# Attention and feed-forward sandwich on one core: batch 0's key and query writes reordered, one load group put behind a small copy, projections and casts spread over the first blocks

## What is computed

```python
x = x + layernorm(attention(layernorm(x)))
x = x + layernorm(ffn(layernorm(x)))

def attention(x):            # 16 heads of 8 features
    q = x @ Wq + bq
    k = (x @ Wk + bk) @ Wl + bl
    v = (x @ Wv + bv) @ Wl + bl
    p = softmax(q @ k.T / sqrt(8))        # per head, 512 x 512
    return (p @ v) @ Wo + bo

def ffn(x):                  # x_prev: the tokens moved down by one
    xr, xk = mix(x, x_prev, mu_r), mix(x, x_prev, mu_k)
    return sigmoid(xr @ W_r) * (square(relu(xk @ W_k)) @ W_v)
```

## Time and profile before

| | us |
|---|---|
| median of 3 executions | 261.02 (260.88 to 261.04) |
| the profiled execution | 260.82 |
| its span in the trace | 259.0 |
| PE busy in the span | 243.8 (94%) |
| DVE busy | 201.7 (78%) |
| ACT busy | 176.5 (68%) |
| POOL busy | 97.2 (38%) |

### The profile page before, as it was taken

One profiled execution on the slowest core, in us unless ns is written; L12 is line 12 of the kernel. 1 busy time (PEld: TensorE's weight loads), 2 busy tenths in 40 slices (PEclk: granted clock), 3 DMA queues, 4 the chain that ended last, 5 costly groups with the idle time before them and its releaser, 6 DMA issues.

```text
span 259.0 us, 4266 instructions
## 1 busy us (share of the span) xinstructions
PE 243.8 (94%) x1359; PEld 91.7 (35%) x1359; DVE 201.7 (78%) x363; ACT 176.5 (68%) x344; POOL 97.2 (38%) x228
## 2 busy tenths in 40 slices
PE   8999979999999999999999999999999999899980
PEld 3554432223222242234322522343224323332560
DVE  3795988778888799879699899796898997721665
ACT  2565868778776866787677767866777677686122
POOL 5948772010101105641216255512153545117322
PEclk9999999999999999999999999999999999999997
DMA  5345765303030303030304130303031000000101
GB/s 162 86 141 158 210 177 168 87 9 93 2 95 2 92 9 87 4 89 4 91 4 94 42 91 4 91 2 94 4 91 42 3 2 0 7 0 0 43 0 41
DMA packets 13816, 15.68 MB, mean 61 GB/s; under 512 B 3153, under 2 KB 11346, under 8 KB 13794
## 3 DMA queue, kind: packets, MB, share of 16 engines
q1 hardware_dynamic: 13218, 15.15, 21.6%
q10 hardware_dynamic: 576, 0.26, 0.4%
HBM read 11.01 MB, written 4.19 MB: 59 GB/s over the span
## 4 chain that ended last, share of the span: by engine, by line
PE 78%; DVE 10%; issue 3%; POOL 3%; ACT 2%; DMA 1%; POOLq 0%; DVEq 0%; ACTq 0%
PE psO L1327 23%; PE psB L1315 21%; PE psA L1296 18%; DVE mx L957 6%; PE psM L1210 3%; PE psM L1216 2%; PE psM L1196 2%; DMA x_all<-in_L_attn_x_dram 1%; PE psO L1234 1%; PE psM L1243 1%; POOL mm L509 1%; PE psM L1276 1%; PE psA L1196 1%; PE psB L1505 1%; PE psM L1256 1%
## 5 line engine op out<-in xcount | busy, mean ns | idle before, releaser
L957 DVE TENSOR_REDUCE mx<-psA 128x2 f32<-128x1024 f32 x128 | 151.1, 1219 | 31.0 <-PE psA L1296 30.6
L809 ACT ACTIVATE pT<-psB 128x512 f32<-128x512 f32 x244 | 132.9, 596 | 39.9 <-PE psB L1315 39.6
L1315 PE MATMUL psB<-QS,KS 75*128 75x512 bf16 x244 | 92.6, 383 | 0.8 <-ACT pT L809 0.3
L1296 PE MATMUL psA<-KS,QS 72*128 72x512 bf16 x256 | 86.7, 379 | 0.4 <-DVE mx L957 0.3
L1327 PE MATMUL psO<-pT,Vg 128*32 128x512 f32 x512 | 68.2, 604 | 0.4
L1315 PEld LDWEIGHTS psB<-QS,KS 75*128 75x128 bf16 x244 | 23.2, 97 | 82.8 <-ACT pT L809 60.8
L1296 PEld LDWEIGHTS psA<-KS,QS 72*128 72x128 bf16 x256 | 24.8, 98 | 18.9 <-DVE mx L957 3.0
L509 POOL TENSOR_TENSOR mm<-mx,one 128x16 bf16<-128x16 f32 x16 | 3.5, 218 | 39.4 <-DVE mx L957 39.4
L1327 PEld LDWEIGHTS psO<-pT,Vg 128*32 128x32 f32 x512 | 10.2, 107 | 18.2 <-issue 13.4
L549 POOL TENSOR_TENSOR Vg<-v_st,one 128x128 f32<-128x128 f32 x16 | 6.3, 402 | 26.4 <-PE psO L1327 26.4
L1196 PE MATMUL psA<-warm 128*128 128x512 bf16 x33 | 9.9, 448 | 1.6 <-DVE warm L921 1.2
(11 more groups left out here) (183 smaller groups left out, 265.4 us busy)
## 6 DMA issues: line engine op xcount, KB each, us to landing
KS<-k_scr SPq DMA_DIRECT2D x45, 96.0 KB
QS<-q_scr SPq DMA_DIRECT2D x15, 288.0 KB
k_scr<-kp SPq DMA_DIRECT2D x12, 128.0 KB, 2.3
q_scr<-qp SPq DMA_DIRECT2D x12, 128.0 KB, 2.4
x_all<-in_L_attn_x_dram SPq DMA_DIRECT2D x4, 256.0 KB, 3.4
out_dram<-out_sb SPq DMA_DIRECT2D x3, 256.0 KB, 2.3
KS<-k_scr SPq DMA_DIRECT2D x6, 48.0 KB
QS<-q_scr SPq DMA_DIRECT2D x2, 144.0 KB
```

What stands on the lines that cost most here:

```text
L809: nc.scalar.activation(pT[:, n % 2, i, :], score_bank(n, i, last), ACT.Exp, scale=SCALE).then_inc(e_rdy, 1)
L957: nc.vector.tensor_reduce(out=mx[:, g % 2, c:c + 2], in_=psA[:, u, :, :], axis=AX.X, op=ALU.max).then_inc(a_max, 1)
L1296: score = nc.tensor.matmul(psA[:, u, j, :], QS[g][0:ROWS, h, P * t:P * (t + 1)], KS[g][0:ROWS, h, :], start=True, stop=True)
L1315: nc.tensor.matmul(score_bank(n, i, last), KS[g][0:KEXP, i, P * t:P * (t + 1)], QS[g][0:KEXP, i, :], start=True, stop=True).then_inc(b_rdy, 1)
```

## The change

On SP: batch 0's third part of the keys is written ahead of the second part of the queries, and group 3's loads stand behind the put of group 0's maxima and a wait for its landing. On PE: batch 1's value projection moves behind the first scores, with three fillers instead of eight ahead of these; the other projections stand at other half steps; the turning of the first maxima comes one half step later; four fillers, into `psO`, stand ahead of the first exponentials' scores, and the wait for `v_tak` moves into block 0. On ACT and POOL: the order of the copies follows, and batch 3's second parts are cast behind the exponentials of blocks 0 and 1. At the end: one filler fewer, and `r` of the first half ahead of the second half's key product, with ACT's order to match.

```diff
-            for i in range(PARTS):
-                write_k(0, i)
-                write_q(0, i)
+            write_k(0, 0)
+            write_q(0, 0)
+            write_k(0, 1)
+            write_k(0, 2)
+            write_q(0, 1)
+            write_q(0, 2)
...
-            for g in range(2, NG):
-                load_k(0, g)
-                load_q(0, g)
+            load_k(0, 2)
+            load_q(0, 2)
             put_maxima(0, 0)
+
+            sp.wait_ge(m_in, 16)
+            load_k(0, 3)
+            load_q(0, 3)
             for b in range(2, NB):
                 write_parts(b)
...
-            split_qk(2)
+            rests_qk(2)
             split_maxima(0, 0)
-            split_qk(3)
+            thirds_qk(2)
+            rests_qk(3)
+            thirds_qk(3)
...
-                            (second_k, 1), (take_q, 2), (take_k, 2), (take_v, 2), (second_q, 2),
-                            (take_xT, 3), (second_k, 2), (take_q, 3), (take_k, 3),
-                            (take_first_maxima, 0), (take_v, 3), (second_q, 3), (second_k, 3)):
+                            (second_k, 1), (take_q, 2), (take_k, 2), (take_xT, 3), (take_v, 2),
+                            (second_q, 2), (take_q, 3), (second_k, 2),
+                            (take_first_maxima, 0), (take_k, 3), (take_v, 3)):
...
                     exponentials(b, n, 3, last)
+                    if first and n < 2:
+                        (second_q, second_k)[n](NB - 1)
...
             z_take_x1T(0)
+            z_take_k(0)
             z_take_x1T(1)
-            z_take_k(0)
+            z_take_r(0)
             z_take_k(1)
-            z_take_r(0)
             z_take_r(1)
...
             job_q(1)
             job_k(1)
-            job_v(1)
-            keep_warm(8)
+            keep_warm(3)
             pe.wait_ge(s_wtc, 3)
 
-            LEAD_JOBS = {(0, 0): (("xT", 2),),
+            LEAD_JOBS = {(0, 0): (("v", 1),),
+                         (0, 1): (("xT", 2),),
                          (1, 0): (("q", 2),),
                          (1, 1): (("k", 2),),
-                         (2, 0): (("v", 2),),
-                         (2, 1): (("xT", 3),),
+                         (2, 0): (("xT", 3),),
+                         (2, 1): (("v", 2),),
                          (3, 0): (("q", 3),),
-                         (3, 1): (("k", 3),),
+                         (4, 0): (("k", 3),),
                          (5, 0): (("v", 3),)}
...
-                    if a == GH and u == 1:
-                        pe.wait_ge(xT_tak, NB)
-                        job_m(0, psB[:, 0, :].bitcast(bf16))
...
                     for job, e in LEAD_JOBS.get((a, u), ()):
                         {"xT": job_xT, "q": job_q, "k": job_k, "v": job_v}[job](e)
-            pe.wait_ge(v_tak, NB)
+                    if a == GH and u == 1:
+                        pe.wait_ge(xT_tak, NB)
+                        job_m(0, psB[:, 0, :].bitcast(bf16))
+            pe.wait_ge(q_tak, 2 * NB)
+            keep_warm(4, psO[:, :])
             pe.wait_ge(m_tak, 1)
...
                     for_maxima(0, 0)
+                    if first and n == 0:
+                        pe.wait_ge(v_tak, NB)
                     for_exponentials(1)
...
-            keep_warm(2, psM[:, :])
+            keep_warm(1, psM[:, :])
...
             z_product_k(0)
             z_x1T(1)
+            z_product_r(0)
             z_product_k(1)
-            z_product_r(0)
```

More of the change, by code:

```diff
@@ L528, in scale_and_shift, with rests_qk @@
                 nc.gpsimd.tensor_tensor(nb[:, :], nm[:, :], rs[:, :], ALU.mult).then_inc(b_sem, 1)
-            def split_qk(b):
+            def rests_qk(b):
                 for full, rest, parts, taken, r1, p2 in ((qf, qr, qp, q_tak, q_r1, q_p2),
@@ L537, in split_qk, with thirds_qk @@
                                             ALU.subtract).then_inc(r1, 1)
+            def thirds_qk(b):
                 for rest, parts, p1, p2 in ((qr, qp, q_p1, q_p2), (kr, kp, k_p1, k_p2)):
@@ L589, in _ @@
             rstd_x(3)
-            split_qk(1)
+            rests_qk(1)
+            thirds_qk(1)
             pool.wait_ge(v_tak, 1)
```

## The result

| | median, us | range | executions |
|---|---|---|---|
| before | 261.03 | 260.88 to 265.48 | 6 |
| changed | 264.6 | 262.04 to 264.97 | 6 |

The ratio is 1.0103, with a 95% interval of 1.0064 to 1.0141: the changed kernel is slower. Its executions do not agree with each other, which is part of the finding. One took 262.04 at a mean granted clock of 0.994, the others 263.2 to 264.97 at 0.981 to 0.988. The profiled one took 264.97, with a span of 263.1, and is one of these. (The ratios and intervals in this document leave out executions over 1.5% slower than the fastest of their kernel; here these are executions in which the clock fell, so the ratios understate such losses: the plain quotient of these medians is 1.0137.)

A forecast was written before the change was run, and what follows sets the result against it. PE's pace from block 4 on was taken to bound the kernel. +1.54 at block 4 and -0.15 at the end gave +1.4: profiled 260.82 to 262.2, median 262.4, range 261.4 to 264.2.

The forecast's parts named there:

- What bounds the kernel: From block 4 on, blocks run at PE's pace; whatever delays block 4 of batch 0 delays the end equally.
- Batch 0's writes and the chain of maxima: Lead-in: first scores at 21.05, 0.54 earlier; eighth maximum ends at 31.7; first put at 33.5, bounds 33.1 and 34.0.
- Up to block 3: Blocks 0 to 3: block 0 at 35.9, 0.9 earlier; PE reaches block 4 at 47.3; spread casts cost nothing.
- SP's queue: First put to block 4: 16.2 us instead of 13.8, so block 4 starts at 49.7, 1.5 later.
- the slow row: Twelfth write's landing: 3.7 us instead of 2.3, block 4 at 51.1, whole ending 1.4 later than forecast.
- The end: After the last blocks: one filler less and the new order save 0.15 us, between 0 and 0.3.
- The size: Whole kernel: median 262.4 us, given 0.78.
- the second rival: At block 4: PE's clock falls in the new wait of about 2.4 us; time 264.4; chance 0.08.
- the cold start: Nine fillers took 4.02 there, eight take 1.89 at full clock; about 4 us at half pace lose 2 us.
- The first rival: At block 4: second put not held by the writes, block 4 0.9 earlier, time 260.0; chance 0.08.

The follow-up runs named there:

- the casts ahead of block 0: Changed kernel without the landing wait, second put ahead of the waits for the writes, batch 3's two casts back ahead of the first exponentials: median 263.45 us.

## Why the prediction was right or wrong

**What bounds the kernel.** Right. The end moved with block 4 in every profile in which the clock held after it: from block 4 to the end of the span it is 210.5 to 210.6 us with the new end, with block 4 anywhere from 46.93 to 49.66.

**Batch 0's writes and the chain of maxima.** Right in kind: first scores at 20.89 (21.05 forecast, 0.70 earlier and not 0.54), first put at 33.53 (33.5).

**Up to block 3.** Right: block 0 at 36.04 (35.9), and PE was ready for block 4 at 47.4 (47.3). To cost the spread casts at nothing was right for the sum, since the wait at block 4 covered them. But I saw them only as two more instructions in the blocks. Their old place costs 1.2 us where that cover is gone, and in most executions more through the clock.

**SP's queue.** Right, term by term: loads at 35.92 (35.8 worked out), twelfth write at 45.02 (45.0), second put at 47.48 (47.4), block 4 at 49.74 (49.7). The twelfth write landed at the 2.3 of the earlier trace rows, so writes behind the loads did not land late, and the slow row did not decide here. The rule of the Trainium skill, "DMA: Bandwidth & Descriptors", section "Queues, rings and completion order", by which a completion counts only after earlier writes, did not decide here either. A put close behind the loads, which took 3.29 instead of 2.36 to release PE, is in line with it, but no run shows that this is the mechanism. I had left that cost out, since the put was not hurt in the trace of before.

**The end.** 0.26 and not 0.15 shorter, inside the range of that term. The mis-sized part is how much of the filler's 0.2 and of the new order survives to the output; how it divides between them stays open.

**The size.** Wrong at the median. The forecast of 262.4 is about the time of an execution in which the clock holds: 262.04 and 261.81, one in each group of runs. The median, 264.6, lies 0.4 above the range's upper end of 264.2. Before's 261.02 times the ratio of 1.0103 gives 263.7, which is inside, but that is luck: 263.7 is a mixture of executions with and without a fall, and the working had only the second kind.

The step that failed is the chance of the second rival, 0.08. The median is that rival's (264.4), with the shift of block 4 as forecast beneath it. I wrote "Before the wait PE is dense, which speaks against it". The clock fell all the same in 16 of 18 executions, and with the wait filled in none of 12. The trace of before had told me that PE's clock outlived 2.6 us without work at its end, and I took that as a sign that 2.4 us are harmless. It is none: in one profile of the changed kernel the fall came after 1.9 us of the wait, in the other 2.2 us after the wait was over. Its price was mis-sized as well: 2.0 was taken from the cold start, and 6.8 us at half pace cost 2.81.

The Trainium skill, "TensorE: Matmul & The Clock Gate", section "HAM oscillation — how this bites in real kernels", on waits for DMAs after which a group of products starts at the low clock, describes this kernel better than I credited. The second profile agrees: the products behind the wait started at half the clock. In the first one they ran at the full clock for 2.2 us, and only then did it fall.

**The first rival, the puts in time.** Not what the change does, but the runs made it real: with the second put ahead of the waits block 4 starts at 46.93 and the median is 259.38. I had priced it at 260.0.

## What to carry to other kernels

Where a string of work at one engine's pace begins behind a DMA, follow the issuing queue to that DMA and add up every issue and every wait in front of it: here each step could be read from the trace of before to 0.2 us, and what helped most was to let the small urgent transfer pass waits it does not need. An idle stretch of PE must be priced twice, as time and as a chance that the clock falls afterwards; ten products of zeros in the stretch cost nothing here and took the second price away. And a median over few executions of such a kernel says little, so look at each execution's granted clock first.

## What was not expected of the hardware

- An idle stretch of PE of 1.23 us, with shorter ones around it, was followed by a fall to half the clock in a profile (the casts ahead of block 0), and one of 2.35 us in 16 of 18 executions. In the five profiles with a fall it came between 0.5 us before the work resumed and 2.8 us after, and lasted 3.4 or 6.8 us.
- The kernel before has the same fall in 43 of 102 executions, with 261 us without it and mostly 264 to 266 with it. With 1.2 us of its lead-in filled with six products it was 1 in 12.
- A put of 12 KB that took 2.36 us from issue to the product that waits for it took 3.29 when it followed four loads of a group by 1.6 us instead of 2.2 (one profile of each).
